# Narrower score units in the band layer, and VectorE's masked keys in two signalled pairs

## The reference

```python
n = S // 64                                   # blocks of 64 queries
k2 = concat([k_of_previous_block, k_of_block])    # 128 keys for 64 queries
valid = (ki >= qi + 1) & (ki <= qi + w)       # w = 64
scores = where(valid, q @ k2.T / 4, -1e30)
out = softmax(scores) @ v2
```

## Time and profile before

| | |
|---|---|
| median of three timed runs | 262.0 us (261.93 to 263.06) |
| the profiled execution | 262.35 us |
| its span | 260.6 us |
| granted TensorE clock | 1.0 of 2.4 GHz in every slice |
| TensorE, VectorE, ScalarE, GpSimd busy | 93%, 79%, 67%, 32% of the span |
| band pair 1, band pair 2 | about 43 to 69 us, 69 to 100 us |
| causal pair 1, causal pair 2 | 100 to 131 us, 131 to 161.5 us |
| mixture of experts | 161.5 us to the end |

### The profile page before, as it was taken

The page is one execution under the profiler, slowest core; times in us unless marked ns, Lnnn a source line. Parts: engine busy times, 40 slices in busy tenths (PEclk is TensorE's granted clock), DMA queues, the critical chain, the costliest instruction groups (busy, mean ns, idle before and its releaser), DMA issues.

```text
span 260.6 us, 4634 instructions
## 1 busy us (share of the span) xinstructions
PE 241.5 (93%) x1545; PEld 179.1 (69%) x1547; DVE 205.5 (79%) x532; ACT 175.3 (67%) x500; POOL 83.6 (32%) x151
## 2 busy tenths in 40 slices
PE   7999879789998999989899898998999999999994
PEld 2787556556765666667576666786788788888882
DVE  3775759976699697987989677579599889599985
ACT  2276344599678976799777986953865395677750
POOL 5200113988898773966540310002200000000000
PEclk9999999999999999999999999999999999999999
DMA  6900000003531320000000000401111000621101
GB/s 196 347 20 3 0 1 0 0 3 87 153 86 27 77 65 0 0 3 0 1 3 1 3 0 3 163 17 28 40 42 43 0 0 20 192 75 40 42 0 40
DMA packets 9318, 11.84 MB, mean 45 GB/s; under 512 B 704, under 2 KB 5952, under 8 KB 9168
## 3 DMA queue, kind: packets, MB, share of 16 engines
q1 hardware_dynamic: 8864, 11.23, 14.1%
q10 hardware_dynamic: 432, 0.33, 0.4%
HBM read 11.00 MB, written 0.56 MB: 44 GB/s over the span
## 4 chain that ended last, share of the span: by engine, by line
PE 52%; DVE 29%; ACT 12%; issue 4%; DMA 1%; POOL 1%; DVEq 0%; SPq 0%; ACTq 0%
DVE negmax L1096 6%; ACT prob L483 5%; PE bank L726 4%; PE bank L674 4%; PE bank L702 4%; PE bank L975 4%; PE bank L972 4%; PE bank L973 4%; PE bank L960 4%; PE bank L962 4%; PE bank L961 4%; PE bank L742 3%; DVE hlo L1350 2%; DVE kM L1084 2%; ACT hb L615 2%
## 5 line engine op out<-in xcount | busy, mean ns | idle before, releaser
L483 ACT ACTIVATE prob<-bank,negmax 128x256 f32<-128x256 f32 (+1 forms) x128 | 52.6, 434 | 8.5 <-DVE negmax L1096 8.3
L615 ACT ACTIVATE hb<-bank,pk 128x512 f32<-128x512 f32 x64 | 42.7, 709 | 17.9 <-PE bank L962 17.9
L1350 DVE TENSOR_TENSOR hlo<-hb,hhi 128x512 fp32r<-128x512 f32 x64 | 42.7, 689 | 12.0 <-ACT hhi L618 10.9
L1096 DVE TENSOR_REDUCE negmax<-bank 128x2 f32<-128x512 f32 (+1 forms) x48 | 32.6, 686 | 12.4 <-PE bank L708 12.3
L726 PE MATMUL bank<-pk,prob 128*128 128x128 f32 x192 | 29.5, 278 | 6.0 <-ACT prob L483 3.3
L726 PEld LDWEIGHTS bank<-pk,prob 128*128 128x128 f32 x192 | 21.8, 142 | 10.9 <-ACT prob L483 5.8
L483 ACT ACTIVATION_READ_ACCUMULATOR prob<-bank,negmax 128x1 f32 x128 | 28.1, 220 | 0.0
L348 POOL TENSOR_TENSOR rstd<-ve,neghalf 128x2 f32<-128x2 f32 x16 | 11.5, 728 | 50.8 <-DVE ve L1057 50.8
L960 PE MATMUL bank<-xhi,w_hi 128*128 128x512 f32 x64 | 25.4, 397 | 0.2
L972 PE MATMUL bank<-hhi,w_hi 128*128 128x512 f32 x64 | 25.3, 395 | 0.0
L450 ACT ACTIVATE probT<-bank 128x512 f32<-128x512 f32 x38 | 22.7, 613 | 3.6 <-PE bank L726 3.3
(11 more groups left out here) (149 smaller groups left out, 487.6 us busy)
## 6 DMA issues: line engine op xcount, KB each, us to landing
w_raw<-w SPq DMA_DIRECT2D x16, 256.0 KB, 3.1
comb_b<-routes SPq DMA_DIRECT2D x16, 256.0 KB, 3.4
pk<-packed SPq DMA_DIRECT2D x1, 1408.0 KB, 9.3
pk<-packed SPq DMA_DIRECT2D x1, 560.0 KB, 6.0
xs<-x SPq DMA_DIRECT2D x3, 128.0 KB, 3.0
out<-acc SPq DMA_DIRECT2D x3, 128.0 KB, 1.7
xs<-x ACTq DMA_DIRECT2D x1, 128.0 KB, 3.2
out<-acc ACTq DMA_DIRECT2D x1, 128.0 KB, 1.8
```

What stands on the lines that cost most here:

```text
L483: last = nc.scalar.activation(prob[n][:, u % 2, i * width:(i + 1) * width], lane[n][u % 2][:, i * width:(i + 1) * width], ACT.Exp, bias=ne ...
L615: nc.scalar.activation(hb[blk % 2][:, j, :], h_bank[j][:, :], ACT.Relu, bias=bias).then_inc(h_ready, 1)
L1096: V.tensor_reduce(negmax[n][:, unit_query(u), heads[0]:heads[-1] + 1], lane[n][u % 2][:, :].rearrange("q (h k) -> q h k", h=len(heads)), A ...
L1350: V.tensor_tensor(hlo[blk % 2][:, j, :], hb[blk % 2][:, j, :], hhi[blk % 2][:, j, :].bitcast(F32), ALU.subtract).then_inc(hlo_ready, 1)
```

## The change

It has three parts.

1. In the band layer, the units of the second query tile use keys 64 to 255 alone (`BAND_FROM`, `unit_keys`): the products, the largest values and the exponentials are 2 x 192 columns in place of 2 x 256. The transposes and `mix` keep their widths, so the columns of `prob` for keys 0 to 63 must be zero. GpSimd sets them once (`zero_unseen`), as soon as the first attention's transposes have read `prob`; ScalarE waits for that ahead of the first two such units. For the zeros to stay, the units of the first query tile get a buffer of their own (`early_prob`, one for each image of a pair), and the others alternate between the two halves of `prob`. The causal layer keeps its widths.
2. VectorE makes its four masked heads with two operations of two heads (a product of two tensors, one repeated over the heads, the other over the keys) where it made four with a scalar operand. The first stands right behind the lower part of the first image's keys, the second behind that of the second image.
3. `kM_ready` and `kM_act_ready` count pairs of heads: TensorE's unit 0 waits for one pair, unit 1 for both. ScalarE makes the pair that its image's unit 0 needs first.

```diff
--- before.py
+++ after.py
@@ -20,6 +20,7 @@
 HP = 32
 HG = 4
 SQ = 16
+BAND_FROM = 64
 PW = WW + 2
 E, HID = 8, 512
 HC = HID // 128
@@ -155,6 +156,7 @@
         w_lo += [sb(f"w_lo{e}", [128, 2, HID], F32R) for e in range(E // 2, E)]
 
         prob = each("prob", [128, 2, 512], scope=attention_memory)
+        early_prob = each("early_prob", [128, 512], n=2, scope=attention_memory)
         probT = each("probT", [128, 2, 512], scope=attention_memory)
 
         first_memory = ExitStack()
@@ -213,6 +215,8 @@
         av_full, rb_ready, rT_full, rT_ready, attn_ready, wo_full, t_ready = (
             sem(n) for n in ("av_full", "rb_ready", "rT_full", "rT_ready", "attn_ready", "wo_full", "t_ready"))
 
+        unseen_zeroed = sems("unseen_zeroed")
+
         s_full, max_ready, exp_done, pT_full, pT_ready = (
             sems(n) for n in ("s_full", "max_ready", "exp_done", "pT_full", "pT_ready"))
 
@@ -281,6 +285,16 @@
 
             query, heads = SCORE_BANKS[u]
             return [h ^ (2 * (n % 2)) for h in heads] if query == 1 else list(heads)
+
+        def prob_of(n, u):
+
+            if unit_query(u) == 0:
+                return early_prob[n % 2]
+            return prob[n][:, sum(unit_query(v) for v in range(u)) % 2, :]
+
+        def unit_keys(a, u):
+
+            return slice(BAND_FROM if (a, unit_query(u)) == (0, 1) else 0, unit_width(u))
 
         def unit_width(u):
 
@@ -377,6 +391,12 @@
                     pool.wait_ge(ve_ready, 2 * j + p + 1)
                     of = slice(ns[0], ns[-1] + 1)
                     G.tensor_tensor(grstd[:, of], gve[:, of], neghalf[:, of], ALU.pow).then_inc(rstd_ready, 1)
+
+            def zero_unseen(n):
+
+                pool.wait_ge(pT0_full, n + 1)
+                G.memset(prob[n][:, 0:2, :].rearrange("q b (h k) -> q (b h) k", k=T)[:, :, 0:BAND_FROM], 0.0
+                         ).then_inc(unseen_zeroed[n], 1)
 
             def split_weights(e):
 
@@ -407,6 +427,8 @@
                 G.tensor_scalar(w_eff[:, :], w_eff[:, :], w_mean[:, 1:2], 1.0, ALU.mult, ALU.mult
                                 ).then_inc(w_eff_ready, 1)
 
+            for n in range(B):
+                zero_unseen(n)
             for n in range(B):
                 power(0, n)
             for p, (a, ns) in enumerate(PHASES):
@@ -469,20 +491,25 @@
             def masked_keys(a, n):
 
                 act.wait_ge(k_parts_ready, a * B + n + 1)
-                for h in range(HG):
-                    last = copy(kM[n % 2][:, h, :], k_parts[n % 2][:, 0, :].bitcast(F32), const("headmask", h, h + 1))
-                last.then_inc(kM_act_ready, 1)
+                for pair in range(2):
+                    for h in unit_heads(n, 2 * pair):
+                        last = copy(kM[n % 2][:, h, :], k_parts[n % 2][:, 0, :].bitcast(F32),
+                                    const("headmask", h, h + 1))
+                    last.then_inc(kM_act_ready, 1)
 
             def exps(a, n, u):
                 act.wait_ge(max_ready[n], a * UNITS + u + 1)
                 if u >= 2:
 
                     act.wait_ge(pT_full[n], a * UNITS + u - 1)
-                width = unit_width(u)
+                if a == 0 and u < 3 and unit_query(u) == 1:
+
+                    act.wait_ge(unseen_zeroed[n], 1)
+                width, keys = unit_width(u), unit_keys(a, u)
                 for i, h in enumerate(unit_heads(n, u)):
+                    of = slice(i * width + keys.start, i * width + keys.stop)
                     last = nc.scalar.activation(
-                        prob[n][:, u % 2, i * width:(i + 1) * width],
-                        lane[n][u % 2][:, i * width:(i + 1) * width], ACT.Exp,
+                        prob_of(n, u)[:, of], lane[n][u % 2][:, of], ACT.Exp,
                         bias=negmax[n][:, unit_query(u), h:h + 1], accum_out=sums[n][:, unit_query(u), h:h + 1])
                 last.then_inc(exp_done[n], 1)
 
@@ -686,7 +713,9 @@
             def scores(a, n, u):
                 if u == 0:
                     pe.wait_ge(q_lo_ready, a * B + n + 1)
-                    pe.wait_ge((kM_ready, kM_act_ready)[n % 2], (a * B + n) // 2 + 1)
+                if u in (0, 1):
+
+                    pe.wait_ge((kM_ready, kM_act_ready)[n % 2], 2 * ((a * B + n) // 2) + u + 1)
                 if u == SECOND_HALF:
                     pe.wait_ge(kM2_ready, a * B + n + 1)
                 if u == 1:
@@ -696,14 +725,15 @@
                     pe.wait_ge(exp_done[n], a * UNITS + u - 1)
                 width = unit_width(u)
                 i, heads = unit_query(u), unit_heads(n, u)
-                dst = lane[n][u % 2]
+                keys = unit_keys(a, u)
+                dst = lane[n][u % 2][:, :].rearrange("q (h k) -> q h k", k=width)
                 g = heads[0] // HG
                 for part in (q_hi, q_lo):
-                    mm(dst[:, :], part[n % 2][:, g, i * 128:(i + 1) * 128],
-                       kM[n % 2][:, heads[0]:heads[-1] + 1, 0:width],
+                    mm(dst[:, :, keys], part[n % 2][:, g, i * 128:(i + 1) * 128],
+                       kM[n % 2][:, heads[0]:heads[-1] + 1, keys],
                        start=(part is q_hi), stop=False, skip_group_check=True)
-                seen = slice(128, T) if (a, i) == (1, 1) else slice(0, width)
-                dst = dst[:, :].rearrange("q (h k) -> q h k", k=width)[:, :, seen]
+                seen = slice(128, T) if (a, i) == (1, 1) else keys
+                dst = dst[:, :, seen]
                 mask = A_MASK[a][i][:, seen].unsqueeze(1).to_broadcast(list(dst.shape))
                 mm(dst, ident_bf, mask, start=False, stop=True, skip_group_check=True).then_inc(s_full[n], 1)
 
@@ -724,7 +754,7 @@
                     pe.wait_ge(ffn_copied if aside == 1 else lg_ready, other(n) + 1)
                 for i in range(4):
                     last = nc.tensor.transpose(lane[n][2][:, i * 128:(i + 1) * 128],
-                                               prob[n][:, u % 2, i * 128:(i + 1) * 128], ident)
+                                               prob_of(n, u)[:, i * 128:(i + 1) * 128], ident)
                 last.then_inc(pT_full[n], 1)
 
             def mix(a, ns, u):
@@ -1077,13 +1107,16 @@
                                        float(HD) ** -0.5, q_hi[n % 2][:, :, :].bitcast(F32), ALU.mult, ALU.subtract
                                        ).then_inc(q_lo_ready, 1)
 
-            def masked_keys(a, n):
+            def masked_keys(a, n, pair):
 
                 dve.wait_ge(k_parts_ready, a * B + n + 1)
-                for h in range(HG):
-                    last = V.tensor_scalar(kM[n % 2][:, h, :], k_parts[n % 2][:, 0, :].bitcast(F32),
-                                           const("headmask", h, h + 1), None, ALU.mult)
-                last.then_inc(kM_ready, 1)
+                first = unit_heads(n, 2 * pair)[0]
+                heads = slice(first, first + 2)
+                shape = [128, 2, T]
+                V.tensor_tensor(kM[n % 2][:, heads, :],
+                                k_parts[n % 2][:, 0:1, :].bitcast(F32).to_broadcast(shape),
+                                const("headmask")[:, heads].unsqueeze(2).to_broadcast(shape), ALU.mult
+                                ).then_inc(kM_ready, 1)
 
             def copy_values(a, n):
                 dve.wait_ge(atv_full, a * B + n + 1)
@@ -1094,7 +1127,7 @@
                 dve.wait_ge(s_full[n], a * UNITS + u + 1)
                 heads = unit_heads(n, u)
                 V.tensor_reduce(negmax[n][:, unit_query(u), heads[0]:heads[-1] + 1],
-                                lane[n][u % 2][:, :].rearrange("q (h k) -> q h k", h=len(heads)),
+                                lane[n][u % 2][:, :].rearrange("q (h k) -> q h k", h=len(heads))[:, :, unit_keys(a, u)],
                                 AX.X, ALU.max, negate=True).then_inc(max_ready[n], 1)
 
             def best_experts(h):
@@ -1322,9 +1355,10 @@
                     for n in ns:
                         inverse_sums(PHASES[p - 1][0], other(n))
                 lower_keys(a, ns[0])
+                masked_keys(a, ns[0], 0)
                 lower_queries(a, ns[0])
                 lower_keys(a, ns[1])
-                masked_keys(a, ns[0])
+                masked_keys(a, ns[0], 1)
                 lower_queries(a, ns[1])
                 if p == 0:
                     for n in PAIRS[1]:
```

## The result

| | before | changed |
|---|---|---|
| median, us | 261.97 (261.87 to 263.06, 4 runs) | 264.65 (263.94 to 265.52, 4 runs) |
| ratio to before | | 1.0089, 95% interval 1.0052 to 1.0127 |
| profiled execution / its span, us | 262.35 / 260.6 | 263.94 / 262.1 |
| mean granted clock of TensorE | 1.00 | 0.991 |

The change is slower by 2.7 us between the medians, by 2.3 us by the ratio; 261.7 was forecast, with a range up to 263.4.

A forecast was written before the change was run, and what follows sets the result against it. GpSimd's full queue was taken to bound the kernel up to 83 us, then VectorE, then TensorE. Gains 0.41 + 0.68 + 0.30 less 0.92 and 0.15 gave 0.32 us: median 261.7 us, 8-in-10 range 260.2 to 263.4.

The forecast's parts named there:

- Part 3: Up to band pair 2's norm: work 2.6 us sooner mostly waits for GpSimd's roots; 0.41 us gained (0.3 to 0.46).
- the gate: GpSimd's two inverse roots in band pair 2, at 83.06 us, for which VectorE's `ht` and then TensorE wait.
- Part 6: At the front, GpSimd's four memsets start with VectorE's `hn` and may hold it: 0.15 us lost (0 to 0.5).
- Part 5: Before the gate, VectorE's two-head key operations hold GpSimd up: 0.92 us net loss (bounds -0.15 to 2.61).
- rival B: Before the gate, VectorE's new operations hold GpSimd for all their time: 2.61 us of delay, 263.4 us; chance 0.13.
- Part 4: Behind the gate, fewer keys save TensorE 0.16 us and four shorter largest values save VectorE 0.52: 0.68 us gained.
- Part 2: VectorE's two-head masked keys: 1.1 us sooner in band pair 1; 0.15 us gained per causal pair, 0.30 together.
- C: The gate does not bind, GpSimd not being in the way: some 3.6 us gained, 258.4 us; chance 0.05.

The follow-up runs named there:

- the common order: GpSimd's first-norm roots ahead of any split, experts 6 and 7 split last: kernel before 262.95 us, change with memsets also later 260.08 us.
- both better orders: Change with memsets later and first-norm roots before splits: experts 6 and 7 split in last phase, 260.08 us; or one split behind second norm's roots, 260.09 us.
- the roots first: The change with only GpSimd's two inverse roots of band pair 2 put ahead of expert 4's split: 263.81 us.
- the fills: Kernel before with five added GpSimd fills of a spare tile ahead of the two inverse roots of band pair 2: 265.65 us.

## Why the prediction was wrong

**The step that failed is the end of Part 3.** It found the gate, its cause and the idle time behind it ("VectorE is to stand idle there for some 3 us"; 3.62 measured), and priced that time at nothing, as work that would have been early anyway. It says that TensorE's transposes wait as well, but not how long TensorE stands idle, nor what that does to its clock. TensorE's 3.03 us of waiting were followed by 3.4 us at half clock, 1.60 us of time, and in the variant with the memsets later by 6.8 us and 2.47. The kernel before kept a mean clock of at least 0.997 in 79 of 84 executions (the other five, at 0.992, took 263.0 to 263.3 us) and 1.00 in the profiled one, so its trace held no price for it, and no rival had one. Holding the clock takes 1.5 to 1.7 us off by the ratios (1.0024 against 1.0082 and 1.0089); making the kernel before wait there brings it about.

**Part 6 is the second miss.** The mechanism (a held `hn`) was named, and 0.15 us taken with a bound of 0.5; 0.71 in the profile and 0.6 by itself. I bounded it by about one memset, and `hn` stood behind all four.

**Part 5 had the place and nearly the size, the size by some luck:** 0.92 forecast, 1.15 in the profile: 0.45 in the masked keys of band pair 1, less 0.11 in the binarized weight, 1.08 in the splits, less 0.27 between the splits and the roots. Three operations held by a pair make 0.43 + 0.34 + 0.41 of it, where 3 x 0.34 was forecast. But the 0.34 was taken as a property of the pair of engines. The rows show the exclusion of rival B, for VectorE's whole operation but its last 0.14 us; it cost less than 0.69 each time because GpSimd's operations started 0.14 to 0.34 us behind VectorE's, and nearly nothing (0.06) at the first pair. Another 0.3 us came from the two `rb` copies, which the forecast doesn't have, and the 0.11 and 0.27 went against it.

**Part 4** gave 0.33 instead of 0.68. Each shortened largest value takes 0.55 instead of 0.69 us, as forecast, but up to the second norm's first root the chain got only 0.06 shorter (12.87 less 12.64, less Part 3's 0.17), since `fz` took 0.59 instead of 0.30 and `ve` 0.46 instead of 0.33; the other 0.27 came up to the second root:

```profile
93.28 0.56 DVE negmax L1129
...
94.20 0.59 DVE fz L1223
...
97.09 0.46 DVE ve L1087
```

**Part 3's own gain** was 0.17 instead of 0.41: roots to turn took 1.50 us instead of 1.67. **Part 2** in the causal pairs: 0.28 and 0.23 us, 0.51 instead of 0.30. In band pair 1 it gave less than its 1.1 us. Counted from `grstd`, the second image's `q_lo` starts at 16.61 us against 16.44, and the first exponential at 19.61 against 19.17; less the 0.71 of the memsets that is 0.54 and 0.27 us sooner, not "about a microsecond". None of it would have passed the gate.

With the clock at 1.60 and the memsets at 0.71 in place of 0 and 0.15, the sum of the prediction, 0.32 us of gain, turns into a loss of 1.84; the other misses, 0.23 in Part 5 and 0.59 in Parts 3 and 4, less 0.21 in Part 2, bring it to the 2.45 of the profile.

Of the rivals, B had the sign, the place and the way in which VectorE holds GpSimd, but its 2.61 us of delay were 1.15, and the loss that brings the time past its 263.4 us is the clock, which it doesn't have. C's 3.6 us for the case that GpSimd is not in the way is what the 2.87 of the common order comes near to.

## What to carry to other kernels

Work that gets early and has to wait is not free of price: ask which engine stands idle and for how long, and if it is TensorE, whether the time behind it is at full clock. Before making the other engines faster, look for the engine whose queue has no gap ahead of a gate (here 33.39 of 36.60 us), and move its deferrable work behind the gate first; then see what the moved work runs beside, since both better orders here gave back about 1 us in the place to which they took the splits. Short fills count where they run, not by how long they are.

## What was unexpected in the hardware

- TensorE's granted clock went to 0.50 for 3.4 or 6.8 us at waits of 2.1 to 3.1 us that stood between busy stretches. In the change, in its second profile and with the roots first, it fell 1.2, 0.35 and 1.0 us after the wait had ended; with the memsets later and with the fills it fell in the wait, 1.5 and 0.7 us before its end. At waits of 1.1 us it stayed at 1.00 in the profiles, and at 1.34 us too, in a kernel whose mean clock was under 0.997 in seven of twelve executions.
- Four memsets of 0.31 us on GpSimd, 0.25 us from start to start, held one VectorE `hn` (0.42 us alone) for 1.13 us in some executions and for 0.61 in others of the same kernel.
- A multiplication of VectorE with two SBUF inputs (0.69 to 0.82 us) delayed GpSimd by 0.34 to 0.52 us, each time by what was left of it less 0.14 us, and so did the one-input `rb` copies (0.28 and 0.14 us in the change). Two one-input operations for the same keys delayed it by next to nothing (3.81 against 3.77 us for eight operations); VectorE waited instead (1.15 us for two of them beside the splits, 0.62 for two ahead of GpSimd's keys).
